# Two fused layers: operands of the first batch stored in halves, and diagonal score blocks added onto a mask that ScalarE has written into PSUM

## What is computed

```python
# layer 0
h_t = tanh(h_prev @ A + u_t @ Bm)          # scan of 512 steps, state 64
y_t = g_t * (h_t @ C.T + u_t @ D.T) + (1 - g_t) * x_t
s = ys @ W_out + b_out + x
c = ft * c + it * gt                       # gated cell, carried over the first axis
g = tanh(x @ wo.T + c_final @ uo.T + bo)
# layer 1: causal attention with 16 heads of 16, and two of 32 low-rank experts per token
scores = einsum('bhqd,bhkd->bhqk', q, k) * hd ** -0.5
scores = where(causal, scores, -inf)
out = einsum('bhqk,bhkd->bhqd', softmax(scores), v)
d2 = |x|^2 + |p|^2 - 2 x @ prototypes.T    # top 2 of softmax(-sqrt(d2) / temp)
y = A[idx] @ (B[idx] @ x) + bias[idx]
```

## Time and profile before

| what | value |
| --- | --- |
| median of 3 runs | 1059.08 us (1058.23 to 1061.97) |
| the profiled execution | 1062.24 us |
| its span (first to last instruction) | 1060.4 us |
| TensorE busy | 1008.4 us, 95% |
| TensorE weight loads | 687.8 us, 65% |
| VectorE busy | 506.2 us, 48% |
| ScalarE busy | 508.2 us, 48% |
| GpSimd busy | 193.4 us, 18% |
| mean granted TensorE clock | 0.984 |
| chain that ended last | TensorE 84%, VectorE 5%, ScalarE 3% |

### The profile page before, as it was taken

How to read it: one execution, slowest core, us unless ns; L and a number is a source line. 1 busy time by engine, 2 the same in 40 slices (tenths; PEclk the granted TensorE clock), 3 DMA queues, 4 the chain that set the end, 5 groups by cost and what they waited for, 6 DMA issues and landing times.

```text
span 1060.4 us, 20152 instructions
## 1 busy us (share of the span) xinstructions
PE 1008.4 (95%) x6546; PEld 687.8 (65%) x6546; DVE 506.2 (48%) x1167; ACT 508.2 (48%) x1378; POOL 193.4 (18%) x225
## 2 busy tenths in 40 slices
PE   5999999999999988899999999999999999999986
PEld 3677777777778863564765765765765665665653
DVE  5031123312134464565665665665665566565541
ACT  3344454444444332465465465465465465454433
POOL 5020111101011013213213213213204204200000
PEclk9999999999999996999999999999999999999989
DMA  8422111103100155241451451351362262234110
GB/s 258 146 73 67 59 49 65 45 31 130 38 30 31 41 182 96 100 121 31 135 154 30 123 163 32 107 172 39 96 176 46 78 186 53 70 102 89 31 41 21
DMA packets 66440, 93.79 MB, mean 88 GB/s; under 512 B 11872, under 2 KB 52832, under 8 KB 66400
## 3 DMA queue, kind: packets, MB, share of 16 engines
q1 hardware_dynamic: 60128, 88.83, 29.7%
q10 hardware_dynamic: 6272, 4.46, 1.3%
HBM read 59.41 MB, written 33.59 MB: 88 GB/s over the span
## 4 chain that ended last, share of the span: by engine, by line
PE 84%; DVE 5%; ACT 3%; issue 2%; DMA 1%; ACTq 1%; SPq 0%; POOL 0%; DVEq 0%; POOLq 0%
PE PS L865 26%; PE PS L1146 7%; PE PS L1043 6%; PE PS L1095 6%; PE PS L1076 5%; PE PS L1111 5%; PE PS L852 4%; PE PS L1009 3%; PE PS L1177 3%; DVE nm L1943 3%; PE PS L988 2%; PE PS L1030 2%; PE PS L1097 2%; PE PS L1133 2%; PE PS L1155 1%
## 5 line engine op out<-in xcount | busy, mean ns | idle before, releaser
L865 PE MATMUL PS<-arena 128*128 128x256 f32 x1024 | 314.1, 421 | 0.0
L1943 DVE TENSOR_REDUCE nm<-PS 128x1 f32<-128x512 f32 (+3 forms) x352 | 207.2, 636 | 92.5 <-PE PS L1097 92.4
L1498 ACT ACTIVATE arena<-PS 128x512 f32<-128x512 f32 x256 | 152.2, 600 | 171.7 <-PE PS L1133 170.5
L1344 ACT ACTIVATE arena<-PS 64x8 f32<-64x8 f32 x512 | 88.1, 172 | 193.3 <-PE PS L852 189.9
L852 PEld LDWEIGHTS PS<-arena 128*72 128x72 f32 x1024 | 129.4, 141 | 69.5 <-ACT arena L1344 6.6
L865 PEld LDWEIGHTS PS<-arena 128*128 128x128 f32 x1024 | 155.5, 192 | 0.0
L1111 PE MATMUL PS<-Q,K 98*128 98x512 bf16 (+3 forms) x512 | 120.6, 301 | 8.7 <-ACT arena L1498 4.6
L852 PE MATMUL PS<-arena 128*72 128x8 f32 x1024 | 122.2, 191 | 0.0
L1095 PE MATMUL PS<-K,Q 96*128 96x256 bf16 (+3 forms) x512 | 114.2, 306 | 6.2 <-DMA K<-qk_d 4.5
L1713 DVE SCALAR_TENSOR_TENSOR arena<-arena 128x512 f32<-128x512 f32 x16 | 11.1, 694 | 224.3 <-ACT arena L1355 224.3
L1097 PE MATMUL PS<-negmask,identb 128*128 128x128 bf16 (+2 forms) x352 | 87.4, 248 | 0.0
(11 more groups left out here) (233 smaller groups left out, 1294.8 us busy)
## 6 DMA issues: line engine op xcount, KB each, us to landing
qk_d<-QB SPq DMA_DIRECT2D x24, 512.0 KB, 3.1
Q<-qk_d SPq DMA_DIRECT2D x32, 192.0 KB, 3.7
K<-qk_d SPq DMA_DIRECT2D x32, 192.0 KB, 4.2
gt_d<-arena SPq DMA_DIRECT2D x16, 256.0 KB, 2.5
wx_d<-arena SPq DMA_DIRECT2D x16, 256.0 KB, 2.4
XT<-xt_d SPq DMA_DIRECT2D x8, 512.0 KB, 4.6
GT<-gt_d SPq DMA_DIRECT2D x8, 512.0 KB, 5.9
WX<-wx_d SPq DMA_DIRECT2D x8, 512.0 KB, 6.7
```

Of the source, the lines that this page charges most:

```text
L865: mm = pe.matmul(o, lhs, rhs, start=first, stop=last, skip_group_check=True)
L1344: s_.activation(HB[0:ST, nxt], PS[0:ST, 7, 0:B], ACT.Tanh).then_inc(c_h.sem, 1)
L1498: s_.activation(PR[:, g % 2, j, at:at + T], PS[:, bank, :], ACT.Exp, scale=SCORE_SCALE).then_inc(t_e.sem, 1)
L1943: v_.tensor_reduce(nm[:, g, h:h + n, i], PS[:, u % 3, 0:n * (i + 1) * P].rearrange("p (n w) -> p n w", n=n), AX.X, ALU.max, negate=True).t ...
```

## The change

1. **Score units.** A unit is now one pair of key tile and query tile for all four heads: four products of 128 columns with four different weights (`UNITS`). The six off-diagonal units use bank 3, the four diagonal ones (0, 3, 6, 8) bank 4. Diagonal products add onto what stands in the bank (`start=False`). `write_edge` on ScalarE writes the mask there again after each diagonal exponential: after the side steps of units 0, 3 and 6, directly behind the exponential of unit 8. `edge_bank` does it the first time, by a product. A unit waits for the last use of its own bank.
2. **Lead-in.** The first halves of the split operands are stored during the last scan step (`save_first(0)`), the second halves behind them. Group 0's key loads are issued by ScalarE, its query loads by SyncE. `distance` and 4 more filler products stand ahead of the waits; GpSimd's `roots` comes before `add_final`; `choose(0)` comes behind the first maxima; ScalarE's `normal_again` comes first and two `hidden` steps later.
3. **Stages.** `distance` moves from unit 9 of stage 1 to stage 2, behind `values`; `take_distance` on VectorE to step 3 of stage 2; `take_query_key(3)` ahead of `middle(0)`. In the first stage 0, `value` moves to units 6 and 7, and on VectorE ahead of `gather_statistics`.

```diff
-PU = P_AT[2]
+UNITS = ((0, 0), (0, 1), (0, 2), (1, 1), (0, 3), (1, 2), (2, 2), (1, 3), (3, 3), (2, 3))
+EDGES = tuple(n for n, (kt, q) in enumerate(UNITS) if kt == q)
-TQ = 5 * GH // 2
+TQ = len(UNITS)
-FILL = (5, 12, 10)
+FILL = (5, 12, 4, 10)
...
+            def save_first(late):
+                to = slice(late * HALF, (late + 1) * HALF)
+                for n in range(SPLIT):
+                    if late:
...
+                    elif n == 0:
+                        sp.wait_ge(f_q, 4)
+                    sp.dma_start(qk_d[n, :, :, :, to].rearrange("c d h t -> (c d h) t")
+                                 .rearrange("(m p) t -> p m t", p=P), QB[:, n, :, to]
+                                 ).then_inc(q_st.sem if late else f_st, 16)
...
             save_half(B // 2 - 1, 0, 1)
+            save_first(0)
             save_half(B // 2 - 1, 1, 1)
...
-            for n in range(SPLIT):
-                save_operands(0, n)
-            for g in range(G):
-                if g == 2:
-
-                    sp.wait_ge(m_ld[0].sem, m_ld[0].at(0, 2))
+            save_first(1)
+            sp.wait_ge(f_st, 16 * SPLIT)
+            sp.wait_ge(q_st.sem, q_st.at(0, SPLIT))
+            for at, n in BLOCKS:
+                load_part(sp, 0, at, n, 0)
+            load_operands(0, 1, False)
+            sp.wait_ge(m_ld[0].sem, m_ld[0].at(0, 2))
+            for g in range(2, G):
                 load_operands(0, g, False)
...
             def turned(b, g, k):
...
-                pe.wait_ge(t_e.sem, t_e.at(b, g * TQ + k - 1))
...
-                n = edge.shape[1]
-                pe.matmul(edge, identb[:, :], negmask_t[:, :].unsqueeze(1).to_broadcast([P, n, P]),
-                          start=False, stop=True).then_inc(t_mm.sem, 1)
+                kt, q = UNITS[k]
+                edge = kt == q
+                before = [n - TQ * (n >= k) for n in range(TQ) if (UNITS[n][0] == UNITS[n][1]) == edge]
+                pe.wait_ge(t_e.sem, t_e.at(b, g * TQ + max(before) + 1))
+                for j in range(GH):
+                    h = g * GH + j
+                    mm = pe.matmul(PS[:, 3 + edge, j * P:(j + 1) * P], K6[0:KM, h, kt * P:(kt + 1) * P],
+                                   Q6[0:KM, h, q * P:(q + 1) * P], start=not edge, stop=True,
+                                   skip_group_check=True)
+                mm.then_inc(t_mm.sem, 1)
...
-                    side[9] = [lambda: distance(b + 1)]
                 stage(b, 1, side, (b, 2))
...
             def stage2(b, more):
                 side = {0: [lambda: values(b, 1)], 2: [lambda: values_turn(b, 1)]}
+                if more:
+                    side[0].append(lambda: distance(b + 1))
...
+            def write_edge(b, g, k):
+
+                act.wait_ge(t_x.sem, t_x.at(b, g * len(EDGES) + EDGES.index(k) + 1))
+                s_.copy(PS[:, 4, :].rearrange("p (j q) -> p j q", q=P),
+                        negmask_t[:, :].unsqueeze(1).to_broadcast([P, GH, P])).then_inc(t_e.sem, 1)
...
             def stage(b, g, side):
                 for k in range(TQ):
                     exp(b, g, k)
+                    if k == EDGES[-1]:
+                        write_edge(b, g, k)
                     run(side, k)
+                    if k in EDGES[:-1]:
+                        write_edge(b, g, k)
...
             early_square(1)
             open_gate(1)
-            second_odds(0)
-            for n in range(3):
-                hidden(1, n)
             for half in range(2):
                 normal_again(1, half)
+            act.wait_ge(f_st, 16 * SPLIT)
+            act.wait_ge(q_st.sem, q_st.at(0, SPLIT))
+            for at, n in BLOCKS:
+                load_part(act, 0, at, n, 1)
+            second_odds(0)
+            hidden(1, 0)
             maxima_high(0, 0)
             take_maxima(0, 0)
+            for n in range(1, 3):
+                hidden(1, n)
```

More of the change, by code:

```diff
@@ L263, in two_layers @@
         f_q = sem("f_q")
+        f_st = sem("f_st")
         w_p = sem("w_p")
@@ L322, in two_layers @@
         t_e = count("t_e", TU, 2)
+        t_x = count("t_x", G * len(EDGES), 1)
         o_mm = count("o_mm", G, 2)
@@ L332, in two_layers, with load_part @@
         z_o = dcount("z_o", 1)
+        def load_part(queue, g, at, n, c):
+            heads = slice(g * GH, (g + 1) * GH)
+            first = PAIRS[at][0]
+            parts = qk_d[0:n, 1] if c else qk_d[first:first + 1, 0].broadcast_to([n, HD, H, T])
+            queue.dma_start((K6 if c else Q6)[at * HD:(at + n) * HD, heads, :],
+                            parts[:, :, heads].rearrange("r d h t -> d r h t")).then_inc(q_ld[g].sem, 16)
         x_v = a["L0_attn_x"].rearrange("b (j p) d -> b p j d", p=P)
@@ L1106, in maxima_turn, with edge_bank @@
                              ).then_inc(m_t.sem, 1)
-            def turned_tile(h, kt, bank, at, first):
-                w = T - kt * P
-                pe.matmul(PS[:, bank, at:at + w], K6[0:KM, h, kt * P:(kt + 1) * P],
-                          Q6[0:KM, h, kt * P:T], start=first, stop=False)
+            def edge_bank():
+                pe.wait_ge(c_w.sem, c_w.at(B, 0))
+                pe.matmul(PS[:, 4, :].rearrange("p (n w) -> p n w", n=GH), identb[:, :],
+                          negmask_t[:, :].unsqueeze(1).to_broadcast([P, GH, P]), start=True, stop=True)
             def turned(b, g, k):
@@ L1213, in stage0 @@
                     side[7].append(lambda: project(b - 1, 1))
-                side[8].append(lambda: value(b, 0, first))
-                side[9].append(lambda: value(b, 1, first))
+                side[6 if first else 8].append(lambda: value(b, 0, first))
+                side[7 if first else 9].append(lambda: value(b, 1, first))
                 stage(b, 0, side, (b, 1))
@@ L1996, in stage0 @@
                 stage(side, (b, 1))
-                if not first:
-                    finish(b - 1, 0)
+                if first:
+                    for p in range(2):
+                        value(b, p)
+                    gather_statistics(b + 1)
+                    return
+                finish(b - 1, 0)
                 if more:
                     gather_statistics(b + 1)
-                if not first:
-                    finish(b - 1, 1)
+                finish(b - 1, 1)
                 value(b, 0)
```

65 lines of the change are left out of this document (25 added, 40 removed).

## The result

| | before | after |
|---|---|---|
| median (runs) | 1060.38 us (4: 1058.23 to 1061.97) | 1072.88 us (4: 1069.00 to 1076.14) |
| profiled execution | 1062.24, span 1060.4 | 1070.07, span 1068.0 |
| mean granted clock of the profiled execution (of all four) | 0.984 | 0.981 (0.973 to 0.981) |

The ratio is 1.0119, with a 95% interval of 1.0091 to 1.0147: the change makes the kernel 1.2% slower. The forecast was 1062 and the range reached to 1076.

The account below looks back on a forecast made before the run. TensorE was taken as the bound, with ScalarE's exponentials one step behind. Steady batches +4, lead-in with next border -5, tail +3, single clock falls +1 sum to +3: 1065 from the profiled 1062.24, 1062 against the median; range 1043 to 1076.

Parts of the forecast that it names:

- the rival on the clock: Steady batches: the clock falls at TensorE's new waits, 1.7 us each, once per batch +12, giving 1074; chance 0.18.
- Masks and fine products: Score stages: mask products go, scores become 40 products 0.055 us apart; TensorE saves 0.83 us per stage, 3.3 per batch.
- the weight-load rival: Score products: 99 ns weight loads do not overlap the product before, +0.9 us per stage, +28 in all, 1090; chance 0.06.
- Copies: ScalarE: four mask copies per stage at 0.6 us each, bounds 0.3 and 0.7; hidden as work, not as latency.
- Borders: Stage borders: TensorE waits for ScalarE's chain, +1.6 (1 to 2), +0.6 (2 to 3), +1.3 us (3 to 0) per batch.
- the rival in which the saving stays on TensorE: Steady batches: ScalarE runs ahead or waits fall where TensorE stands anyway; 1048, or 1035 with no give-back; chance 0.28.
- Lead-in: Before the steady part: early stores and two load queues start scores 3.2 to 3.6 us earlier; -2.5, or -7 at high clock.
- the next border: After the lead-in: value copies ahead of statistics remove a 2.32 us wait, unit 2 waits for GpSimd's chain; -1.7 us.
- my mark of 397: Lead-in: scores starting at 397 would show the prediction right; first scores later than 399 would show it wrong.
- Tail: Last stage: 11.1 us between the last value products against 9.1, and possible low clock; together +3 us.
- single falls of the clock in the steady part: Steady batches: occasional drops of TensorE's clock, booked at +1 us in all.

Follow-up runs that it names:

- e4: The changed kernel with TensorE writing unit 0's bank by one 512-column product, without the copy behind unit 8; three copies stay: 1059.49 us, 0.9990 of before.
- e2: The kernel before with the score units and ScalarE's mask copies alone, lead-in and distance as before: 1072.63 us, 1.0161 of before.
- e5: The changed kernel with 512-column filler products at five places where TensorE waits: 1070.63 us, 1.0106 of before.
- e7: e4 with nine filler products per batch, and two behind each unit of the last stage: 1063.39 us, 1.0031 of before.
- e8: e4 with whole rows in the last batch's last stage, and stage 3's row-maxima transfers issued ahead of a low-rank copy: 1053.78 us, 0.9923 of before.
- e10: e8 with the distance products back at the end of stage 1, where the kernel before has them: 1055.00 us, 0.9931 of before.
- e3: The changed kernel with distance back at unit 9 of stage 1, take_distance at that stage's end: 1068.32 us, 1.0111 of before.
- e12: e4 with only the early row-maxima transfers of e8; the last stage keeps the new cut: 1056.67 us, 0.9966 of before.

## Why the prediction was right and wrong

It had the direction and the mechanism of the steady batch, and 1072.9 lies within 1043 to 1076. That is owed to the width of the range: 1072.9 is outside the forecast's own 1053 to 1069 and close to the 1074 of the rival on the clock, to which I gave 0.18. Against its own execution it forecast +3 and the profiled execution gave +7.8. The two runs of after whose clock is 0.973 to 0.975 take 6 us more than the two at 0.981.

- **Masks and fine products: right.** The forecast was 3.3 us of TensorE's own path per batch. Its busy time fell by 2.4, with overlapping durations. Products with loads of their own start 0.055 to 0.06 us apart, in groups of four and eight, so the weight-load rival is out. So is, here, the 81 ns that the Trainium skill gives in "TensorE: Matmul & The Clock Gate", section "Back-to-back issue gap", for this kind of stream.
- **Copies: right.** 0.589 us each against 0.6 taken.
- **Borders: right.** The chain of stage 1 to 2 from unit 8 to the value products was worked out as 3.65 and measures 3.66. By stages, stages 1 and 2 together: forecast +0.69 (-1.66 + 1.6 + 0.6 + 0.15), measured +0.84. Stage 3: +0.47 forecast, +0.37 measured. Stage 0: -0.53 forecast, -0.47 measured. The batch: +0.6 forecast, +0.74 measured. So the rival in which the saving stays on TensorE is out. e4 shows that it was open only if the copy behind unit 8 went.
- **Lead-in: right in sum, wrong in its parts.** Forecast -5 with the next border. The first value products came 5.66 earlier. Scores started only 1.6 us earlier, not 3.2 to 3.6: 399.05 is past my mark of 397 and just past 399, which I had named as a sign of being wrong. Both steps of that sum were too large. The first load was issued 1.5 us earlier (392.01 against 393.50), not 2.6. From there to the scores it took 7.04 us against 7.12, so the second queue brought 0.1 and not 1: the six loads were all issued by 394.2 instead of 397.1, but the last of them landed 5.4 us after its issue instead of 3.9. The transfers share the time, and I had counted too little for it. Of the other 4.1 us, 2.3 are the wait of the earlier trace rows that is gone, as I had it, and the rest comes mostly from the low clock, which ended 6.7 us earlier and to which I had given only some chance. The next border was to gain 1.7. The 2.3 came, but the first batch lost 2.93 us (+0.74 of it the steady loss), because unit 2 waits 2.46 us behind the normalisations. I had seen that wait and put it too low. Both together: -5.66 + 2.19 = -3.5.
- **Tail: nearly right.** 11.21 between the last value products against 11.1 forecast; low clock there, as forecast; the whole end +2.13 against +3.
- **The clock: the term that was mis-sized.** I booked +1 for "single falls of the clock in the steady part" and gave the rival with one fall per batch 0.18. The price of a fall was right (4.05 against 2.36 us, 1.7 forecast). The number was not: three in five batches in the profiled execution, +4.6. The slower two runs take 6 us more at a lower mean clock, which would be about four more falls at 1.65 each; no trace of them shows it. I had worked out 1.87 us of waits at one border (1.09 + 0.73 measured), which I named for this rival, and held against it a clock of 1.00 that belonged to the old waits. I had compared it with the lead-in, but there TensorE is busy for 21.24 of 27.30 us, so that row is no measure of such a border. And I had not expected falls at the border of stage 3 to 0, where two of the three falls of after and five of the six of e2 lie. e5 shows that the waits do it, and e2 that units and copies alone, without the moved distance, already bring one fall per batch.

The 7.6 us between the profiled executions are then: -5.7 before the first value products, +2.9 in the first batch, +3.6 in five steady batches without their falls, +4.6 for the falls, and +2.1 behind them. The other 5 us of the median's +12.5 are not traced: 2.8 are the slower runs of after, whose mean clock is lower, and 1.9 the faster runs of before.

## What to carry to other kernels

Work taken off the bounding engine and given to an idle one is paid for in latency wherever the idle engine is one step behind at a border. Follow the queue from the last unit of a stage to what the bound waits for, and leave on the bound the one piece that stands in that chain: here a 0.22 us product instead of a 0.59 us copy turned +0.74 into -0.85 us per batch. When new waits of TensorE come close together (1.1 and 0.7 us, or 1.3 and 0.4, at one border), reckon with falls of the clock there, some 1.5 to 1.7 us a time: here three at ten such places (after), six in five batches (e2), none with waits of 0.5 to 0.7 us (e4). These runs give no way to work out their number beforehand. Filler products prevented them in the steady batches (e5), but can pay only where falls occur; where the waits are as short as half a microsecond they cost more than they gave (e7). Check the first and last turn of a loop apart: both had losses of their own, and mending them in part made e4, level with the kernel before, into e8, 0.8% faster.

## What was not expected of the hardware

- Falls of the clock recur at the same place of the batch, batch after batch (e2, five times, 81.9 us apart), or in every second one (e10), or irregularly (after). The kernels differ by a few tenths of a microsecond in the length of a batch; whether that is what sets the pattern is not shown.
- Covering 0.9 us of waits per batch (e3) went with eight falls instead of three. This stays open.
- A 4 KB transfer landed after 3.4 us beside a fetch of instructions and after 1.8 otherwise. One case only, in the first pass through the loop, and in e12 a fetch in the same stretch did no harm.
- ScalarE can write a bank in PSUM that later products are added onto. The copy from SBUF, 128 x 512 from bf16 to f32, takes 0.589 us, as long as its exponentials of that size (0.598).
